# A decoder layer on one core: layer-norm scalings and hi/lo splits moved from VectorE to ScalarE, and a first body with an order of its own

## The chip, the core and the metric

The kernel runs on one core of one Trainium2 chip. The metric is the device time of one execution in microseconds. A core has TensorE (PE, with its weight loads as PEld), VectorE (DVE), ScalarE (ACT), GpSimd (POOL) and SyncE (SP, which here only issues DMAs). Each engine runs its own list of instructions in order and waits on semaphores.

## What is computed

x is 16 x 56 x 512 in float32, the context is 16 x 1500 x 512. Three residual blocks follow one another, each on a layer-normed x:

```python
x = x + attn(layernorm(x))           # 32 query heads, 8 key/value heads, causal, softmax
x = x + xattn(layernorm(x), ctx)     # latent cross-attention:
#   C_kv = ctx @ Wkv_d               (1500 x 32 per batch)
#   q    = (layernorm(x) @ Wq_d) @ W_qk      (16 heads x 32)
#   out  = softmax(q . C_kv / sqrt(32)) @ (C_kv @ Wv_u)
x = x + ffn(layernorm(x))            # x @ kernel + bias + two low-rank terms
# layernorm(x) = (x - mean) / sqrt(var + 1e-5)
```

## The kernel before

**Units of work.** Two batch elements form a pair (n = 0 to 7), since 2 x 56 rows fill the partitions. Pair n needs one self-attention, one set of cross-attention queries and one feed-forward. Each of the 16 batch elements b needs two passes of cross-attention. The first pass, `maxima(b, p)` on PE (line 754) with `reduce_piece` on DVE (line 1143), makes 21 pieces of scores and their row maxima. The maxima are negated (`NM`, lines 1148 to 1156, seven numbers per partition, split into a high and a low part), transposed (`MT`, line 637), copied by ACT into m_t and sent by two DMAs into rows 96 and 97 of the query operand q_st (`spread_m`, lines 341 and 343). The second pass, `scores(b, g, t)` (line 711), then gives scores with the maximum already subtracted: 24 units per batch element, in 6 groups g of 4. ACT takes the exponential of each unit into one of the 8 slots of p_ring (line 941), POOL adds the slots up into acc (line 1214), and `sums(b, g)` on PE multiplies a group with the context (line 726). The score banks are two (STB = 2), so a score matmul waits for the exponential two units earlier.

**Bodies and groups.** The program is one prologue and nine bodies i = 0 to 8. A body has 12 groups of instructions. In body i PE runs the scores of batch elements 2i-1 (groups 0 to 5) and 2i (groups 6 to 11), the pieces of 2i and 2i+1, and between them the small steps of the list `STEPS`, written out by hand: per group a list of names with a letter that says for which pair or batch element. All engines walk the same list and each does its part of a step. Within a group come first the four score units and the pieces of `PIECES_IN` (one per unit), with the sums of the group before after the second unit, then the steps. On ACT a group is first its four exponentials, then its parts of the steps.

**Steps of the change.** `Ah` and `A` (line 503) compute the transposed latent context C_kv of one batch element from ctx_sb into a PSUM bank. ACT copies the bank to ct_f (line 898, by the helper at line 840). `AS` on DVE makes ct_hl from ct_f: a rounded copy (line 1041) and the remainder (line 1043). SP spreads ct_hl into the operand c_st by 12 DMAs per batch element (`spread_ct`, line 393). `CT` (line 626) transposes ct_f for the sums. `L0`, `W1` and `YT` on DVE end in `statistics` (lines 1010 to 1014), which gives mean and variance; POOL's `power` makes rstd in two instructions (lines 1222 and 1225); `N0`, `N1` and `N2` on DVE normalise x into xn or x3n (line 1018); `T1`, `T2`, `T3` (line 490) transpose the result on PE, and ACT copies that into xnt. `K`, `Qh`, `Q1`, `WA`, `SA`, `WB`, `SB` are the self-attention's projections and scores, `SM0`/`SM1` (lines 1105, 1107), `SE0`/`SE1` (ACT, line 859) and `SN0`/`SN1` (lines 1115 to 1119) its softmax, `V`, `P0` to `P3`, `O1`, `Wh`, `W1` the rest of it; `CQ` and `H` make the cross queries, which SP spreads (line 402). `DN`, `DT`, `Y`, `YT` finish the cross-attention; `F1`, `Fh`, `F2` are the feed-forward.

**Loads.** SP reads the context of a batch element (3 MB, line 375) into one of two slots of ctx_sb. In the prologue it reads elements 0 and 1; element 2 is read at the start of body 0, element 3 after the spread of element 1. ACT issues half of the first queries' spreads (lines 335 to 336) and the two writes of the low-rank factors (line 985) before body 0.

**Line 1266 ff.** POOL's body is `power(0, i+1)`, then the additions of the bodies' units, with `power(1, i+1)` and `power(2, i-1)` between them.

## Time and profile before

| | us |
|---|---|
| median of 3 runs | 643.73 (642.36 to 645.56) |
| the profiled execution | 645.84 |
| its span | 644.0 |
| PE busy | 584.1 (91% of the span) |
| DVE busy | 432.5 (67%) |
| POOL busy | 412.7 (64%) |
| ACT busy | 302.1 (47%) |
| mean granted TensorE clock | 0.968 of full speed |

The profile is of one execution. The span goes from its first to its last instruction, and 1.84 us lie around it. A line of a timeline gives the start in us, the duration in us, the engine, the line of the program, the operation and its tiles, the number of instructions merged in it, and in brackets how long the engine had been idle and what released it. Busy PE time contains the overlap of following matmuls, so stalls are read from the brackets.

### The profile page before, as it was taken

How to read it: one execution, taken by the hardware profiler on the slowest of the kernel's cores; microseconds unless marked ns; L12 is line 12 of the kernel's file. 1: busy time of each engine (PE TensorE's matmuls, PEld its weight loads, DVE VectorE, ACT ScalarE, POOL GpSimd, SP SyncE). 2: the span in 40 equal slices, each digit the busy share in tenths (PEclk: the TensorE clock that was granted, in tenths of full speed). 3: DMA queues.
4: the chain of work that ended last, by engine and by line, in shares of the span. 5: the costliest groups of instructions: out<-in, count | busy, mean ns of one | idle time of the engine just before them, and what ended most of it. 6: DMA issues, size and time to landing. Idle time of an engine off the chain costs nothing.

```text
span 644.0 us, 11508 instructions
## 1 busy us (share of the span) xinstructions
PE 584.1 (91%) x4164; PEld 315.5 (49%) x4164; DVE 432.5 (67%) x715; ACT 302.1 (47%) x642; POOL 412.7 (64%) x385
## 2 busy tenths in 40 slices
PE   7889797998999899999999899998999899988887
PEld 7436353455446354545446355455446355434445
DVE  2737964678757967778747957678757967656632
ACT  1421434537444555437444555437444555464460
POOL 5002166598758887598758887588758887789000
PEclk9997788899999999999999999999999999999899
DMA  9959511651048110751039110761039110200000
GB/s 320 409 107 348 208 36 24 251 206 35 12 120 317 59 45 22 268 204 39 9 108 336 52 45 22 253 219 32 16 93 334 68 45 23 64 19 0 24 2 15
DMA packets 31578, 77.40 MB, mean 120 GB/s; under 512 B 11297, under 2 KB 24961, under 8 KB 29218
## 3 DMA queue, kind: packets, MB, share of 16 engines
q1 hardware_dynamic: 30854, 75.27, 34.9%
q10 hardware_dynamic: 668, 1.40, 0.6%
q8 instruction: 33, 0.54, 0.4%
q14 instruction: 23, 0.19, 0.1%
HBM read 58.92 MB, written 2.88 MB: 96 GB/s over the span
## 4 chain that ended last, share of the span: by engine, by line
PE 58%; DVE 19%; ACT 6%; POOL 4%; SPq 4%; issue 4%; DMA 4%; ACTq 0%; POOLq 0%; DVEq 0%
PE st_ps L711 11%; PE mx_ps L754 9%; PE pv_ps L726 8%; PE mi_ps L496 4%; PE mi_ps L490 4%; DVE mx_p L1143 4%; POOL acc L1214 3%; PE mi_ps L503 3%; DVE p L1066 2%; PE mi_ps L586 2%; SPq L402 2%; DMA ctx_sb<-in_ctx_t 2%; DVE xn L1018 2%; PE mi_ps L590 2%; DVE p L1107 2%
## 5 line engine op out<-in xcount | busy, mean ns | idle before, releaser
L1214 POOL TENSOR_TENSOR acc<-acc,p_ring 125x448 f32<-125x448 f32 x290 | 348.0, 1200 | 65.4 <-ACT p_ring L941 25.8
L1143 DVE TENSOR_REDUCE mx_p<-mx_ps 128x1 f32<-128x500 f32 x336 | 210.0, 669 | 98.9 <-PE mx_ps L754 97.9
L941 ACT ACTIVATE p_ring<-st_ps 125x448 f32<-125x448 f32 x372 | 183.4, 544 | 151.6 <-PE st_ps L711 139.7
L711 PE MATMUL st_ps<-q_st,c_st 98*125 98x448 f32 x372 | 146.3, 432 | 9.8 <-ACT p_ring L941 8.6
L754 PE MATMUL mx_ps<-c_st,q_st 96*128 96x500 f32 x336 | 142.1, 457 | 12.2 <-DVE mx_p L1143 5.1
L711 PEld LDWEIGHTS st_ps<-q_st,c_st 98*125 98x125 f32 x372 | 65.3, 190 | 99.3 <-ACT p_ring L941 79.9
L726 PE MATMUL pv_ps<-p_ring,c_nat 125*32 125x448 f32 x768 | 94.5, 564 | 1.9 <-ACT ox L840 1.0
L754 PEld LDWEIGHTS mx_ps<-c_st,q_st 96*128 96x128 f32 x336 | 63.6, 197 | 43.7 <-DVE mx_p L1143 17.6
L1222 POOL TENSOR_TENSOR rstd<-mv,eps_col 128x1 f32<-128x1 f32 x24 | 4.6, 190 | 117.1 <-DVE mv L1014 116.6
L503 PE MATMUL mi_ps<-ctx_sb,wkv_sb 128*32 128x375 f32 x480 | 46.8, 511 | 5.5 <-DVE p L1066 5.5
L1214 POOL TENSOR_TENSOR acc<-p_ring 125x448 f32<-125x448 f32 x29 | 35.6, 1226 | 19.2 <-ACT p_ring L941 19.2
L1098 DVE TENSOR_TENSOR x3n<-mi_ps,x 128x512 f32<-128x512 f32 x8 | 5.5, 692 | 46.0 <-PE mi_ps L695 46.0
L840 ACT ACTIVATE qt<-mi_ps 128x512 f32<-128x512 f32 x16 | 9.6, 598 | 48.8 <-PE mi_ps L496 44.0
L496 PEld LDWEIGHTS mi_ps<-xnt,wq_sb 128*128 128x128 f32 x256 | 31.1, 193 | 1.7 <-DMA wq_sb<-in_wq 0.8
L496 PE MATMUL mi_ps<-xnt,wq_sb 128*128 128x128 f32 x256 | 31.2, 276 | 0.6 <-DMA wq_sb<-in_wq 0.6
L726 PEld LDWEIGHTS pv_ps<-p_ring,c_nat 125*32 125x32 f32 x768 | 15.5, 109 | 30.4 <-issue 21.8
L859 ACT ACTIVATE p<-p 128x896 f32<-128x896 f32 x16 | 15.2, 951 | 26.4 <-DVE p L1107 26.4
L503 PEld LDWEIGHTS mi_ps<-ctx_sb,wkv_sb 128*32 128x32 f32 x480 | 13.1, 113 | 27.1 <-issue 18.2
L840 ACT ACTIVATE xnt<-mi_ps 128x512 f32<-128x512 f32 x24 | 14.3, 597 | 21.8 <-PE mi_ps L490 21.7
L1066 DVE TENSOR_TENSOR p<-mi_ps,cmask 128x448 f32<-128x448 f32 x32 | 18.4, 618 | 7.4 <-PE mi_ps L560 7.4
L490 PE MATMUL mi_ps<-ident,p 128*128 128x128 f32 x128 | 19.6, 289 | 3.5 <-ACT p1t L840 3.5
L1018 DVE TENSOR_SCALAR xn<-x_sb,mv,rstd 128x512 f32<-128x512 f32 x16 | 19.7, 1230 | 3.6 <-POOL rstd L1225 3.6
(137 smaller groups left out, 677.9 us busy)
## 6 DMA issues: line engine op xcount, KB each, us to landing
ctx_sb<-in_ctx_t SPq DMA_DIRECT2D x16, 3000.0 KB, 11.6
c_st<-ct_hl SPq DMA_DIRECT2D x192, 46.9 KB, 2.3
q_st<-q_hl SPq DMA_DIRECT2D x90, 56.0 KB, 2.0
x_sb<-in_x SPq DMA_DIRECT2D x8, 256.0 KB, 2.8
out_y<-x3n SPq DMA_DIRECT2D x16, 112.0 KB
wq_sb<-in_wq SPq DMA_DIRECT2D x2, 512.0 KB, 6.4
kern_sb<-in_lora_a SPq DMA_DIRECT2D x1, 1024.0 KB, 14.2
wo_sb<-in_wo SPq DMA_DIRECT2D x1, 1024.0 KB, 17.6
```

The costliest lines, as they stand in the source:

```text
L490: last = pe.transpose(bank_[:, c * 128:(c + 1) * 128], src[:, c * 128:(c + 1) * 128], ident[:, :])
L496: last = mm(o[:, r * 128:(r + 1) * 128], wq_sb[:, c, r * 128:(r + 1) * 128], xnt[:, c, :], start=(c == 0), stop=(c == CH - 1))
L503: last = mm(o[t * L:(t + 1) * L, 0:KT], wkv_sb[:, c, :], ctx_sb[:, slot, c, t * KT:(t + 1) * KT], start=(c == 0), stop=(c == CH - 1))
L711: mm(st_bank(unit)[0:KC, 0:HALF], c_st[:, b % 4, t * KT + k * KC:t * KT + (k + 1) * KC], q_st[:, b // 2 % 2, b % 2, half * HALF:(half + 1) ...
L726: last = mm(pv_ps[t * L:(t + 1) * L, 0:HALF], c_nat[:, b % 4, k, t * L:(t + 1) * L], p_ring[:, unit % PR, :], start=(k == 0), stop=(k == K ...
L754: mm(mx_ps[(b * PIECES + p) % MXB][:, 0:KP], q_st[0:96, b // 2 % 2, b % 2, j * 128:(j + 1) * 128], c_st[0:96, b % 4, k * KP:(k + 1) * KP], ...
L840: return act.activation(dst, src, ACT.Copy, scale=scale)
L941: act.activation(p_ring[:, unit % PR, :], st_bank(unit)[0:KC, 0:HALF], ACT.Exp, scale=float(L) ** -0.5).then_inc(exp_done, 1)
L1018: ve.tensor_scalar(dst, src, mv[:, which, 0:1], rstd[:, which, 1:2], ALU.subtract, ALU.mult)\
L1066: ve.tensor_tensor(rows[:, j:j + 2, half, :, 0:S], mi_ps[half][:, 0:G * S].rearrange("p (r g k) -> p r g k", r=2, g=G // 2), mask, ALU.add ...
L1143: ve.tensor_reduce(mx_p[:, p:p + 1], mx_ps[unit % MXB][:, 0:KP], AX.X, ALU.max).then_inc(red_done, 1)
L1214: po.tensor_tensor(dst, first, p_ring[:, unit % PR, :].rearrange("p (h s) -> p h s", s=S), ALU.add).then_inc(acc_done, 1)
```

## The change

- `statistics` gets a third result, the negated mean (one more DVE instruction of one element per partition), and `power` a third POOL instruction, -mean x rstd.
- `N0`, `N1`, `N2` run on ACT as one activation Identity with scale rstd and bias -mean x rstd; only `N0` and `N1` of pair 0, in the prologue, stay on DVE. `N0` keeps its place as the last step of group 0. `N1` stands in group 9 after the third exponential (in body 0 in group 7), `N2` in group 10 after the second.
- The rounded part of ct_hl is a second ACT copy from the bank of `A`; `AS` on DVE is only the remainder, and reads the bank. `AS` of the even batch elements moves from the end of group 5 to group 4, ahead of `SN0`. `CT` on PE waits for the remainder too.
- Body 0 gets its own list `FIRST_STEPS` and its own pieces. Batch element 0's scores start in group 4 (they started in group 6), groups 10 and 11 hold no steps, `Ah` and `A` of element 3 run on PE at the end of body 0 (they ran in group 0 of body 1). `MT` of element 0 uses a score bank, `Ah` and `A` of element 2 the bank of the sums.
- The context of element 2 is read from ACT's queue, behind ACT's spreads and the two writes.

```diff
-FIRST_PIECES_IN = [3, 2, 4, 0, 0, 0, 2, 4, 4, 0, 0, 0]
+FIRST_PIECES_IN = [3, 2, 4, 4, 0, 0, 4, 4, 4, 4, 0, 0]
...
-    [("SE0", "n"), ("Ah", "b"), ("MT", "m"), ("A", "b"), ("SE1", "n"), ("V", "n"), ("SN0", "n")],
-    [("CT", "b"), ("SN1", "n"), ("AS", "b")],
+    [("SE0", "n"), ("Ah", "b"), ("MT", "m"), ("A", "b"), ("AS", "b"), ("SE1", "n"), ("V", "n"),
+     ("SN0", "n")],
+    [("CT", "b"), ("SN1", "n")],
...
-    [("DN", "f"), ("Wh", "n"), ("M", 1), ("W1", "n"), ("M", 1), ("DT", "f"), ("N1", "n")],
-    [("YT", "f"), ("M", 1), ("T2", "n"), ("M", 1), ("CQ", "n"), ("M", 1), ("H", "n"), ("N2", "f")],
+    [("DN", "f"), ("Wh", "n"), ("M", 1), ("W1", "n"), ("M", 1), ("DT", "f")],
+    [("YT", "f"), ("M", 1), ("T2", "n"), ("M", 1), ("CQ", "n"), ("M", 1), ("H", "n")],
...
-FIRST_STEPS = {9: STEPS[9] + [("NM", "o")], 10: [("MT", "o")], 11: []}
+FIRST_STEPS = [
+    [("Ah", "a"), ("A", "a"), ("L0", "n"), ("M", 3), ("AS", "a"), ("N0", "n")],
+    [("CT", "a"), ("M", 1), ("T1", "n")],
+    [("K", "n"), ("M", 1), ("Qh", "n"), ("M", 3), ("Q1", "n")],
+    [("WA", "n"), ("NM", "m"), ("SA", "n"), ("Ah", "b"), ("MT", "m"), ("A", "b"), ("WB", "n"), ("SM0", "n"),
+     ("SB", "n"), ("SM1", "n")],
+    [("AS", "b"), ("SE0", "n"), ("V", "n"), ("CT", "b"), ("SE1", "n"), ("SN0", "n")],
+    [("SN1", "n"), ("P0", "n"), ("P1", "n"), ("P2", "n"), ("P3", "n")],
+    [("O1", "n"), ("M", 1), ("Wh", "n"), ("M", 1), ("W1", "n")],
+    [("M", 1), ("T2", "n"), ("M", 1), ("CQ", "n")],
+    [("H", "n"), ("M", 1)],
+    [("NM", "o"), ("MT", "o")],
+    [],
+    [],
+]
+FIRST_SCORES = 4
...
+def scores_at(i, g):
+    b, k = (2 * i - 1 + g // GROUPS, g % GROUPS) if i else (0, g - FIRST_SCORES)
+    return (b, k) if b < B and 0 <= k < GROUPS else None
+
+def sums_at(i, g):
+    if i == 0:
+        return scores_at(0, g - 1)
+    return None if (i, g) == (1, 0) else scores_at(*((i, g - 1) if g else (i - 1, 2 * GROUPS - 1)))
+
+N1_AT, FIRST_N1_AT = 9, 7
+
+def normal_at(i, g, t):
+    for (gn, tn), name, n in (((N1_AT if i else FIRST_N1_AT, 2), "N1", i + 1), ((10, 1), "N2", i - 1)):
+        if (g, t) == (gn, tn) and 0 <= n < PAIRS:
+            yield name, n
...
+            if n == 0 and name == "MT":
+                return st_ps[0]
+            if n == 2 and name in ("Ah", "A"):
+                return pv_ps
...
             def body(i):
-                if 2 * i + 2 < B:
-                    if i:
-                        load_x(i + 1)
+                if i and 2 * i + 2 < B:
+                    load_x(i + 1)
                     load_ctx(2 * i + 2)
...
                 elif name == "CT":
+                    if n == 2:
+                        pe.wait_ge(s1_sb, 8)
                     pe.wait_ge(a_f, n + 1)
+                    if n:
+                        pe.wait_ge(a_lo, n + 1)
...
                     for name, n in steps_of(i, g):
-                        if name in ("Ah", "A") and n == 1:
+                        if name in ("Ah", "A") and n in (1, 3):
                             continue
                         step(name, n, i, g)
                 if i == 0:
+                    for name in ("Ah", "A"):
+                        step(name, 3)
+                    pe.wait_ge(w_up, 16 * 4)
                     pe.wait_ge(w_ffn, 16 * 3)
                     pe.wait_ge(y_out, 16)
...
+            def normalise(which, n, src, dst):
+                act.wait_ge(ln_shift[which], n + 1)
+                act.activation(dst, src, ACT.Identity, bias=rstd[:, which, 2:3], scale=rstd[:, which, 1:2])\
+                    .then_inc(ln[which], 1)
...
                 elif name == "A":
+                    copy(ct_f[:, :], o[:, 0:KT]).then_inc(a_f, 1)
                     if n:
-                        act.wait_ge(a_lo, n)
-                    copy(ct_f[:, :], o[:, 0:KT]).then_inc(a_f, 1)
+                        act.wait_ge(cst_in[(n - 1) % 4], 16 * 12 * ((n - 1) // 4 + 1))
+                    copy(ct_hl[:, 0, :], o[:, 0:KT]).then_inc(a_hi, 1)
...
+            read_ctx(act.dma_start, 2)
             def body(i):
                 for g in range(2 * GROUPS):
-                    part, gg = g // GROUPS, g % GROUPS
-                    bs = 2 * i - 1 + part
-                    if 0 <= bs < B:
-                        exponentials(bs, gg)
...
+                    ready, summed = scores_at(i, g), sums_at(i, g)
+                    for t in range(4):
+                        if ready:
+                            exponential(*ready, t)
+                        for name, n in normal_at(i, g, t):
+                            step(name, n)
...
-                ve.bn_aggr(mv[:, which, :], stats[:, which, 0:6]).then_inc(s, 1)
+                ve.bn_aggr(mv[:, which, 0:2], stats[:, which, 0:6]).then_inc(s, 1)
+                ve.wait_ge(s, k + 2)
+                ve.tensor_scalar(mv[:, which, 2:3], mv[:, which, 0:1], -1.0, None, ALU.mult).then_inc(ln_neg[which], 1)
...
-                    if n:
-                        ve.wait_ge(cst_in[(n - 1) % 4], 16 * 12 * ((n - 1) // 4 + 1))
-                    ve.wait_ge(a_f, n + 1)
-                    ve.tensor_copy(ct_hl[:, 0, :], ct_f[:, :]).then_inc(a_hi, 1)
                     ve.wait_ge(a_hi, n + 1)
-                    ve.tensor_tensor(ct_hl[:, 1, :], ct_f[:, :], ct_hl[:, 0, :].bitcast(F32), ALU.subtract)\
+                    ve.tensor_tensor(ct_hl[:, 1, :], step_bank("A", n)[:, 0:KT], ct_hl[:, 0, :].bitcast(F32),
+                                     ALU.subtract)\
                         .then_inc(a_lo, 1)
...
                 po.tensor_tensor(rstd[:, which, 1:2], rstd[:, which, 0:1], minus_half[:, :], ALU.pow)\
                     .then_inc(ln_pow[which], 1)
+                po.wait_ge(ln_pow[which], n + 1)
+                po.wait_ge(ln_neg[which], n + 1)
+                po.tensor_tensor(rstd[:, which, 2:3], mv[:, which, 2:3], rstd[:, which, 1:2], ALU.mult)\
+                    .then_inc(ln_shift[which], 1)
```

## Rows read from the trace of the kernel before

**Rows 1.** The page, busy time of each engine over the span.

```profile
PE 584.1 (91%) x4164; PEld 315.5 (49%) x4164; DVE 432.5 (67%) x715; ACT 302.1 (47%) x642; POOL 412.7 (64%) x385
```

**Rows 2.** Windows, bodies 0, 1, 3, 4: length, busy PE PEld DVE ACT POOL, clock, DMA.

```profile
45.60:111.40 65.80, 53.80 (x312) 31.32 (x312) 47.35 (x78) 21.28 (x45) 25.54 (x23) 0.82 0.47 155
111.40:187.30 75.90, 71.81 (x499) 37.86 (x499) 52.24 (x85) 38.33 (x82) 59.57 (x54) 0.96 0.34 115
...
259.20:331.10 71.90, 67.81 (x498) 36.37 (x496) 52.76 (x86) 36.64 (x79) 55.38 (x51) 1.00 0.36 121
331.10:404.80 73.70, 69.52 (x498) 37.27 (x496) 53.03 (x86) 36.85 (x79) 55.36 (x51) 0.98 0.36 118
```

**Rows 3.** Timeline of PE in body 3, four rows before which it stood idle.

```profile
282.17 0.50 PE L754 MATMUL mx_ps<-c_st,q_st 96*128 96x500 f32 x1 [0.63 <-DVE p L1066]
...
286.23 1.47 PE L503 MATMUL mi_ps<-ctx_sb,wkv_sb 128*32 128x375 f32 x16 [0.57 <-DVE p L1066]
...
292.96 0.90 PE L711 MATMUL st_ps<-q_st,c_st 98*125 98x448 f32 x2 [0.92 <-ACT p_ring L941]
...
316.96 0.66 PE L490 MATMUL mi_ps<-ident,xn 128*128 128x128 f32 x4 [0.68 <-DVE xn L1018]
```

**Rows 4.** Groups of instructions over the whole span: count, busy us, mean ns, idle before.

```profile
L1018 DVE TENSOR_SCALAR xn<-x_sb,mv,rstd 128x512 f32<-128x512 f32 x16 | 19.7, 1230 | 3.6 <-POOL rstd L1225 3.6
...
L1043 DVE TENSOR_TENSOR ct_hl<-ct_f,ct_hl 128x375 fp32r<-128x375 f32 x16 | 15.1, 941 | 0.5
...
L840 ACT ACTIVATE x<-x_sb 128x512 f32<-128x512 f32 x8 | 5.0, 628 | 0.0
```

**Rows 5.** Timeline of body 3 around N0, end of group 0 and group 1.

```profile
265.72 0.48 ACT L840 ACTIVATE ct_f<-mi_ps 128x375 f32<-128x375 f32 x1 [2.72 <-PE mi_ps L503]
...
265.81 0.17 DVE L1014 BATCH_NORM_AGGREGATE mv<-stats 128x2 f32<-128x6 f32 x1
...
266.06 0.19 POOL L1222 TENSOR_TENSOR rstd<-mv,eps_col 128x1 f32<-128x1 f32 x1 [6.46 <-DVE mv L1014]
266.10 0.97 ACT L941 ACTIVATE p_ring<-st_ps 125x448 f32<-125x448 f32 x2
...
266.32 0.55 POOL L1225 TENSOR_TENSOR rstd<-rstd,minus_half 128x1 f32<-128x1 f32 x1
...
267.52 0.67 PE L711 MATMUL st_ps<-q_st,c_st 98*125 98x448 f32 x2
...
268.03 0.49 PE L626 MATMUL mi_ps<-ident,ct_f 128*125 128x128 f32 x3
```

**Rows 6.** Timeline of ACT in body 3, the four exponentials of group 5.

```profile
292.37 2.08 ACT L941 ACTIVATE p_ring<-st_ps 125x448 f32<-125x448 f32 x4
```

**Rows 7.** Timeline of body 3 around N1, group 9.

```profile
314.97 0.55 POOL L1225 TENSOR_TENSOR rstd<-rstd,minus_half 128x1 f32<-128x1 f32 x1
...
315.28 0.98 ACT L941 ACTIVATE p_ring<-st_ps 125x448 f32<-125x448 f32 x2 [0.51 <-PE st_ps L711]
```

**Rows 8.** Timeline of SP in body 0, the fourth context read and the first maxima sent.

```profile
59.06 0.58 SPq L375 DMA_DIRECT2D ctx_sb<-in_ctx_t  x1
71.73 1.63 SPq L341 DMA_DIRECT2D q_st<-m_t  x2
```

**Rows 9.** DMA issues from 59.0 to 60.5 us: KB each, us to landing.

```profile
ctx_sb<-in_ctx_t SPq DMA_DIRECT2D x1, 3000.0 KB, 16.0
```

**Rows 10.** Windows, two us at the start of body 1, columns as in rows 2.

```profile
112.00:114.00 2.00, 1.95 (x5) 1.24 (x5) 0.21 (x1) 1.54 (x3) 1.71 (x3) 0.50 0.36 84
```

**Rows 11.** Timeline of PE in body 0 and at the start of body 1, scores.

```profile
75.36 0.45 PE L711 MATMUL st_ps<-q_st,c_st 98*125 98x448 f32 x1
...
84.01 0.58 PE L711 MATMUL st_ps<-q_st,c_st 98*125 98x448 f32 x1
...
111.41 1.93 PE L711 MATMUL st_ps<-q_st,c_st 98*125 98x448 f32 x3 [2.05 <-ACT p_ring L941]
```

**Rows 12.** Waits over the whole span: us in total, times, longest us.

```profile
DVE x3n L1018 <- POOL rstd L1225: 3.8, 2, 2.9
```

More of the change, by code:

```diff
@@ L125, in steps_of @@
     done = sum(pieces_in(i)[g // GROUPS * GROUPS:g + 1])
-    done += sum(w for h in range(g // GROUPS * GROUPS, g) for name, w in STEPS[h] if name == "M")
+    done += sum(w for h in range(g // GROUPS * GROUPS, g) for name, w in steps_in(i, h) if name == "M")
     for name, w in steps_in(i, g):
@@ L160, in pieces_within @@
     done = sum(pieces_in(i)[g // GROUPS * GROUPS:g])
-    done += sum(w for h in range(g // GROUPS * GROUPS, g) for name, w in STEPS[h] if name == "M")
+    done += sum(w for h in range(g // GROUPS * GROUPS, g) for name, w in steps_in(i, h) if name == "M")
     return range(done, done + pieces_in(i)[g])
@@ L280, in decoder_layer @@
         ln_pow = [sem(f"ln_pow{n}") for n in range(3)]
+        ln_neg = [sem(f"ln_neg{n}") for n in range(3)]
+        ln_shift = [sem(f"ln_shift{n}") for n in range(3)]
         st_done = sem("st_done")
@@ L614, in step @@
                 elif name == "Ah":
-                    if n % 2 == 0 and n:
+                    if n % 2 == 0 and n > 2:
                         pe.wait_ge(s1_sb, 2 * n + 4)
@@ L720, in sums @@
                     pe.wait_ge(ct_sb, b + 1)
+                if b == 0 and g == 0:
+                    pe.wait_ge(a_f, 3)
                 if k == 0 and b * 2 + half:
@@ L922, in step, with exponential @@
                     copy(ax_t[0:2 * RANK, :], o[0:2 * RANK, 0:128]).then_inc(f1_sb, 1)
-            def exponentials(b, g):
-                half = g // KG
-                if b == 0 and g == 0:
+            def exponential(b, g, t):
+                unit = b * 24 + g * 4 + t
+                if unit == 0:
                     act.wait_ge(eff_out, 32)
-                for t in range(4):
-                    unit = b * 24 + g * 4 + t
-                    act.wait_ge(st_done, unit + 1)
-                    old = unit - PR
-                    if old >= 0:
-                        act.wait_ge(pv_done, old // 4 + 1)
-                        added = (old // 24, old // 12 % 2)
-                        if added in DVE_HALVES:
-                            act.wait_ge(acc_dve, dve_adds(*added) + max(old % 12, 1))
-                        elif added != PE_HALF:
-                            act.wait_ge(acc_done, pool_adds(*added) + max(old % 12, 1))
-                    act.activation(p_ring[:, unit % PR, :], st_bank(unit)[0:KC, 0:HALF], ACT.Exp,
-                                   scale=float(L) ** -0.5).then_inc(exp_done, 1)
+                act.wait_ge(st_done, unit + 1)
+                old = unit - PR
+                if old >= 0:
+                    act.wait_ge(pv_done, old // 4 + 1)
+                    added = (old // 24, old // 12 % 2)
+                    if added in DVE_HALVES:
+                        act.wait_ge(acc_dve, dve_adds(*added) + max(old % 12, 1))
+                    elif added != PE_HALF:
+                        act.wait_ge(acc_done, pool_adds(*added) + max(old % 12, 1))
+                act.activation(p_ring[:, unit % PR, :], st_bank(unit)[0:KC, 0:HALF], ACT.Exp,
+                               scale=float(L) ** -0.5).then_inc(exp_done, 1)
             def out_of_sums(b, half):
```

64 lines of the change are left out of this document (39 added, 25 removed).

## The prediction

> **What bounds the kernel now.** I read the page first, then the windows body by body, then PE's timeline of one body, then the stretches of the other engines that release it. By the page TensorE is busy 91% of the span and DVE 67% [rows 1], so work taken from DVE is worth only what PE waits for it. The windows show two regimes [rows 2]. Body 3 stands for bodies 2 to 6: 71.9 us, PE busy 67.8, clock 1.00, so some 4 us of stalls each. Bodies 0 and 1 are worse: 65.8 us at a mean clock of 0.82 with 12 us of PE idle, and 75.9 us at 0.96, which is 4.0 longer than body 3. The first body and the entry to the second are where time lies; a steady body has stalls of half a microsecond.
>
> In body 3 the stalls that matter here are before four rows [rows 3]: 0.63 and 0.57 us for the masks' additions of the softmax, 0.92 for the exponentials of group 5, 0.68 for N1's xn. Only the last is a wait for an operation that the change moves. The others keep their releasers.
>
> **What the moved work costs.** On DVE a normalisation takes 1230 ns in the mean, the remainder 941; an ACT pass over 128x512 in SBUF takes 628 [rows 4]. Per steady body DVE sheds N0, N1 and N2, 3.7 us of 52.8, and two CASTs. I price that at nothing by itself: DVE is idle 19 us of a steady body and PE waits for it only at the rows named. It costs something if DVE's work after the moved ones was late for PE; no bracket in body 3 shows that in groups 0 to 2. The added negation on DVE is hidden by POOL's power chain.
>
> **N1, each steady body.** POOL's second instruction ends at 315.52 [rows 7]. The new third one is of the form of the first, 0.19 long and 0.26 after its predecessor with its semaphore [rows 5], so the shift is there at 315.78. ACT starts the third exponential at 315.28 and is free some 0.44 later, so N1 runs from about 315.85 to 316.48 and T2 starts at 316.54 instead of 316.96 [rows 3]. The fourth exponential slips by 0.6, behind YT and T2 on PE, and nothing waits. Gain 0.42 us per body.
>
> **N0, each steady body: a new wait.** N0 is now ahead of group 1's four exponentials in ACT's order. Before, ACT went from the ct_f copy at 265.72 straight to the first exponential at 266.10 [rows 5]. Now the second copy for ct_hl takes that place, and ACT is free at 266.5. N0 waits for POOL: the aggregate ends at 265.98, POOL's second instruction at 266.87, the third at 267.13 [rows 5]. N0 starts at 267.2, and the next ACT instruction 0.52 later (the 628 of rows 4 less some 0.1 of overlap): the first exponential at 267.72 instead of 266.10. A queued exponential is followed by its score matmul 0.59 us after its start: 292.37 [rows 6] and 292.96 [rows 3]. So the third score starts at 268.31 instead of 267.52 [rows 5]. The fourth waits for the second exponential, 0.44 later, 268.75, and CT, 0.27 after it, starts at 269.02 instead of 268.03. PE loses 1.0 us. Bounds: 0 if POOL were so early that the first exponential still started by 266.93; 1.2, what the same pattern cost in group 5 (0.92 and a spacing 0.2 longer). I take 1.0, since every term is a row. Behind ACT nothing else suffers: the CT copy and T1's copy shift by the same 1.0, and POOL's additions start 0.26 later.
>
> **The splits.** In group 4 the second copy falls where ACT waited for SM1, so SE1 and V keep their times. AS in group 4 puts 0.9 us at most [rows 4] ahead of SN0, and PE has group 5's scores and sums before P0 and P2 need SN0 and SN1. SP's 12 DMAs start 5 us earlier; their consumer is a body away. CT's wait for the remainder ends before CT in both halves. All these: 0, at worst 0.3 per body.
>
> **The first body.** Its start is unchanged: DVE reduces the pieces one by one. In the new order T1, K, Q1 come within half a microsecond of where they were, and with all 21 pieces of element 0 ahead of SA, m_t can be issued at about 65.5 by my count instead of 71.73 [rows 8]. But its two DMAs stand on SP's queue behind the fourth context, which was issued at 59.06 and took 16.0 us to land, 75.06 [rows 8, 9], while the first score started at 75.36 [rows 11]. With the third context on ACT's queue SP issues the fourth some 1.6 us earlier (the start of element 1's spread no longer waits for DVE's CAST; my estimate), with the same bytes to move. I put the first scores at 73.5. From there: it was 8.65 us to the next score group at 84.01 [rows 11]; in the new order one more group of four exponentials, 2.08 [rows 6], stands in it, while part of the softmax is done before, 9.5 by my count. From there to body 1 it was 27.4. One group with its sums less is -3.0; five pieces more are +1.2 (an estimate, a piece behind a score costs about half of its 0.50 [rows 3]); Ah and A of element 3 are two times 1.47 [rows 3], +2.9; N1 on ACT is -0.7; the stall of 2.05 before body 1, ACT busy with issuing m_t's DMAs [rows 11], is covered by those Ah and A: 25.8, with a wait for m_in of 0.2. Body 1 would start at 109.0; PE has been idle for five us before 73.5, after which I expect the clock at its lower level for some of group 4, +1.0. So 110.0, 1.4 earlier.
>
> **Body 1** loses Ah and A: 2.9 us at the full clock, up to twice that at the 0.50 that PE had just after the entry [rows 10]; I take 3.3. Body 1 is 4.0 us longer than body 3 [rows 2], which I put down to that clock. With a shorter stall at the entry I take back about half of the remaining 3.6, less a little for doubt: -1.5.
>
> **The end.** The two last N2 wait for POOL [rows 12]; each becomes 0.26 + 0.08 later, +0.6 together.
>
> **Sum**: -1.4 (body 0), -3.3 and -1.5 (body 1), +6.0 (N0, bodies 1 to 6), -2.5 (N1, the same six), +0.6 (end): -2.1 us. The profiled execution took 645.84, 2.1 above the median of 643.73. Against it the sum gives 643.7, against the median 641.6, which is what I forecast. Half a percent, 3.2 us, is about what a measurement of this kernel can tell from no change; the forecast lies inside it.
>
> **Two rules weighed.** The two context reads now lie on two queues. In the trace the third, ahead in one queue, had landed before its use. The Trainium skill, "DMA: Bandwidth & Descriptors", section on queues, rings and completion order, says that each DMA engine goes round-robin between the queues that have work. By it the third context lands later, since the fourth takes half the rate from 57.4 on. That would hold Ah of element 2 by up to 2 us. It falls into the wait for m_t, so the sum stays. The same section says that a DMA's semaphore lands only after every earlier write of that DMA engine, across its queues. By it m_t's rows can't be ahead of the fourth context, and the next rival is excluded; no row of before shows it.
>
> **Rivals.**
> *m_t's rows don't wait* for the fourth context. For: they are 7 KB. Against: 3 MB stand ahead of them in their queue. Then SP's issue from 65.5 to 67.1 and 2 us of landing put the first scores at 69.1: 4.4 earlier, -6.5, 637.2. With the clock full in body 1 it is 1.8 less, 635.4.
> *N0's wait is hidden*, if POOL or the x load is earlier than in body 3: the sum loses 6.0 and is -8.1, 635.6. Against: L0's place in DVE's list is unchanged.
> *The clock falls in the steady bodies* (slower). Body 4 took 73.7 us at a mean clock of 0.98, 1.8 more than body 3 [rows 2]. A fall of that size after the new 1.0 us idle in group 1, in each of the five other bodies 1 to 6, is +9.0, and the sum +6.9, 650.6. It decides from three bodies on (+3.3). For: PE's idle share rises by 1.4% and the falls in bodies 0 and 1 come after stalls. Against: 0.92 and 0.57 close together didn't bring it in body 3.
> *DVE's relief does nothing and body 0 keeps its length*: without -1.4 and -1.5 the sum is +0.8, 644.5.
>
> **How the numbers follow.** Forecast 0.45, own range 638.5 to 645 by the bounds of N0 (0.6 to 1.2 us a body), of body 0 (2 us either way) and of the clock. m_t early 0.18, N0 hidden 0.07, clock 0.17, no gain 0.13. Faster by over 0.5% are the two fast rivals and a third of the forecast: 0.40. Slower by over 0.5% are the clock rival and a little of the others: 0.20. The rest 0.40. The range takes in the fast rivals at 635 and the clock rival in four bodies, 649.
>
> **What would show it.** Per body, right: PE idle before the third score of group 1, released by the exponential behind xn; T2's idle near 0.25; body length 72.5. First score near 73.5, behind the fourth context; body 1 starting near 110 and near 71 long. Wrong: steady bodies under 71.9 (N0 mispriced), a first score before 71, or windows with a clock under 1.00 in bodies 2 to 6.

## The result, and the profile of the changed kernel

The changed kernel takes 649.17 us (median of 5 runs, 648.3 to 650.07), the kernel before 644.93 (median of 5, 642.36 to 646.46): 1.0072 times as long, 95% interval 1.0046 to 1.0098. It is slower by 4.2 us, where 2.1 faster was forecast. The profiled executions stand 2.5 us apart (648.3 and 645.84): the one of before lies 0.9 above its median, the other 0.9 below. The balance by stages below is of these two profiles; 1.7 of the 4.2 us between the medians it can't show.

The page's busy times, which answer to [rows 1]:

```profile
PE 577.3 (89%) x4164; PEld 313.9 (49%) x4164; DVE 404.4 (63%) x701; ACT 323.8 (50%) x680; POOL 416.3 (64%) x409
```

DVE has shed 28 us, ACT took 22 more, and PE stands idle for 9 us more than before (span less busy time). The windows of bodies 0, 1, 3 and 7, in the columns of [rows 2]:

```profile
46.00:114.00 68.00, 52.79 (x354) 30.75 (x355) 43.24 (x76) 25.10 (x52) 31.05 (x29) 0.90 0.46 154
114.00:185.30 71.30, 65.62 (x455) 36.49 (x456) 48.30 (x83) 39.44 (x83) 54.75 (x53) 0.98 0.35 117
258.60:331.20 72.60, 68.14 (x498) 36.49 (x496) 49.03 (x84) 39.66 (x84) 55.40 (x54) 1.00 0.37 120
549.80:609.00 59.20, 52.11 (x295) 24.10 (x293) 36.96 (x64) 30.12 (x63) 39.83 (x37) 0.91 0.08 21
```

Taking the start of body 1's first scores and the start of the last matmul of each pair's F2 as marks, the time stands like this (us; bodies 2 to 6 are five lengths from mark to mark):

| stretch | before | after | difference | forecast |
|---|---|---|---|---|
| to body 1's first scores | 112.63 | 114.00 | +1.4 | -1.4 |
| body 1 | 73.8 | 71.3 | -2.6 | -4.2 |
| bodies 2 to 6 | 362.1 | 363.8 | +1.7 | +2.9 |
| body 7 | 57.6 | 59.1 | +1.4 | together |
| behind it | 33.3 | 33.8 | +0.5 | +0.6 |

(Body 1's forecast is -3.3 and -1.5, with one body's share of N0 and N1, +0.6.) In the kernel before, body 1 starts at 112.63 and not at 111.41, which the prediction takes from [rows 11] for it. The windows of that kernel, with its score matmuls (L711) alone, tell it; the numbers after x are their counts on PE and PEld:

```profile
75.30:111.40 36.10, 8.46 (x22) 4.08 (x22) 0.91 0.10 24
75.30:112.62 37.32, 9.63 (x24) 4.57 (x25) 0.90 0.11 26
```

Element 0 has 24 scores, and only 22 lie before 111.41. That row is the third score of the last group of body 0, and the stall of 2.05 us before it stands inside body 0. The prediction's start of body 1, 110.0, is therefore 111.2 by the true mark; its differences stay. The largest miss is the first body, 2.8 us. The timeline of PE there in the changed kernel, for [rows 11]:

```profile
75.91 1.11 PE L766 MATMUL st_ps<-q_st,c_st 98*125 98x448 f32 x2 [6.91 <-DMA q_st<-m_t]
...
109.56 0.27 PE L692 MATMUL mi_ps<-ident,nm_hl 128*14 128x128 f32 x1 [1.83 <-DVE nm_hl L1232]
...
114.00 0.45 PE L766 MATMUL st_ps<-q_st,c_st 98*125 98x448 f32 x1 [0.76 <-DMA q_st<-m_t]
```

PE stands still for 6.91 us before the first scores, and waits for the two rows of m_t. The timeline of SP and, below, one row of the chain, for [rows 8]:

```profile
59.26 0.58 SPq L387 DMA_DIRECT2D ctx_sb<-in_ctx_t  x1
67.01 1.61 SPq L393 DMA_DIRECT2D q_st<-m_t  x2
...
67.90 7.97 DMA q_st<-m_t
```

m_t is issued at 67.01, 4.7 us earlier than before, but 7 KB take 7.97 us to land: the fourth context, issued at 59.26, takes 16.3 us and lands at 75.5. Of a steady body, the groups 0 and 1 of body 3, for [rows 5]:

```profile
265.28 0.48 ACT L901 ACTIVATE ct_f<-mi_ps 128x375 f32<-128x375 f32 x1 [2.72 <-PE mi_ps L553]
...
265.89 0.55 POOL L1301 TENSOR_TENSOR rstd<-rstd,minus_half 128x1 f32<-128x1 f32 x1
...
266.51 0.19 POOL L1305 TENSOR_TENSOR rstd<-mv,rstd 128x1 f32<-128x1 f32 x1
...
266.74 0.81 ACT L905 ACTIVATE xn<-x_sb,rstd 128x512 f32<-128x512 f32 x1 [0.61 <-POOL rstd L1305]
267.46 0.96 ACT L1012 ACTIVATE p_ring<-st_ps 125x448 f32<-125x448 f32 x2
...
268.04 0.90 PE L766 MATMUL st_ps<-q_st,c_st 98*125 98x448 f32 x2 [0.89 <-ACT p_ring L1012]
```

This is the forecast's picture: ACT waits for POOL's third instruction, N0 stands ahead of the exponentials, and PE loses 0.89 us before the third score.

### The profile page after: what moved, and what is told of

It is laid out like the page before. It is cut to its first block, busy times and chain, and to the rows that moved or that the text cites. A ratio compares the mean times of both kernels' runs of the same rounds, so it can differ in the third digit from the quotient of the medians.

```text
span 646.5 us, 11585 instructions
## 1 busy us (share of the span) xinstructions
PE 577.3 (89%) x4164; PEld 313.9 (49%) x4164; DVE 404.4 (63%) x701; ACT 323.8 (50%) x680; POOL 416.3 (64%) x409
## 3 DMA queue, kind: packets, MB, share of 16 engines
q1 hardware_dynamic: 30710, 72.19, 33.8%
## 4 chain that ended last, share of the span: by engine, by line
PE 56%; DVE 17%; ACT 7%; issue 6%; DMA 6%; POOL 5%; SPq 2%; ACTq 1%; POOLq 0%; DVEq 0%
PE st_ps L766 11%; PE pv_ps L783 8%; PE mx_ps L811 8%; POOL acc L1290 4%; DVE mx_p L1219 4%; PE mi_ps L546 3%; PE mi_ps L540 3%; ACT p_ring L1012 3%; DMA ctx_sb<-in_ctx_t 3%; PE mi_ps L637 2%; DVE p L1183 2%; PE mi_ps L641 2%; PE mi_ps L744 2%; DVE p L1138 2%; DVE sm L1181 2%
## 5 line engine op out<-in xcount | busy, mean ns | idle before, releaser
L766 PE MATMUL st_ps<-q_st,c_st 98*125 98x448 f32 x372 | 148.3, 435 | 23.1 <-ACT p_ring L1012 14.3
L811 PE MATMUL mx_ps<-c_st,q_st 96*128 96x500 f32 x336 | 140.2, 448 | 11.2 <-DVE mx_p L1219 4.8
L766 PEld LDWEIGHTS st_ps<-q_st,c_st 98*125 98x125 f32 x372 | 65.9, 190 | 113.2 <-ACT p_ring L1012 87.7
L1290 POOL TENSOR_TENSOR acc<-p_ring 125x448 f32<-125x448 f32 x29 | 33.1, 1142 | 20.6 <-ACT p_ring L1012 20.6
L553 PE MATMUL mi_ps<-ctx_sb,wkv_sb 128*32 128x375 f32 x448 | 40.6, 483 | 0.0
L783 PEld LDWEIGHTS pv_ps<-p_ring,c_nat 125*32 125x32 f32 x768 | 15.4, 108 | 30.3 <-issue 23.8
L1195 DVE TENSOR_TENSOR p<-p,sm 128x896 f32<-128x896 f32 x16 | 22.5, 1408 | 0.6
L1191 DVE TENSOR_REDUCE sm<-p 128x16 f32<-128x896 f32 x16 | 17.2, 1077 | 7.1 <-ACT p L931 7.0
L540 PE MATMUL mi_ps<-ident,p 128*128 128x128 f32 x128 | 17.9, 275 | 4.0 <-ACT p1t L901 3.6
## 6 DMA issues: line engine op xcount, KB each, us to landing
ctx_sb<-in_ctx_t ACTq DMA_DIRECT2D x1, 3000.0 KB, 16.9
```

What stands on the lines that cost most here:

```text
L540: last = pe.transpose(bank_[:, c * 128:(c + 1) * 128], src[:, c * 128:(c + 1) * 128], ident[:, :])
L553: last = mm(o[t * L:(t + 1) * L, 0:KT], wkv_sb[:, c, :], ctx_sb[:, slot, c, t * KT:(t + 1) * KT], start=(c == 0), stop=(c == CH - 1))
L766: mm(st_bank(unit)[0:KC, 0:HALF], c_st[:, b % 4, t * KT + k * KC:t * KT + (k + 1) * KC], q_st[:, b // 2 % 2, b % 2, half * HALF:(half + 1) ...
L783: last = mm(pv_ps[t * L:(t + 1) * L, 0:HALF], c_nat[:, b % 4, k, t * L:(t + 1) * L], p_ring[:, unit % PR, :], start=(k == 0), stop=(k == K ...
L811: mm(mx_ps[(b * PIECES + p) % MXB][:, 0:KP], q_st[0:96, b // 2 % 2, b % 2, j * 128:(j + 1) * 128], c_st[0:96, b % 4, k * KP:(k + 1) * KP], ...
L1191: ve.tensor_reduce(total, rows, AX.X, ALU.add).then_inc(soft_n, 1)
```

## The experiments

Eleven kernels were run, each timed against the kernel before. Ratios are to that kernel, with 95% intervals; they are not the quotients of the medians and differ from them by up to 0.003 (b3: 633.79 over 644.50 would be 0.983). "Mean of bodies 2 to 6" is that of the five lengths between F2 marks in the profile: 72.77 for the changed kernel and 72.43 for before (its median is 72.12, since one of the five was lengthened by a clock fall). The labels are those of the headings.

**a1, the fourth context behind m_t.**

```diff
-                            if n % 2 and n + 2 < B:
+                            if n % 2 and n + 2 < B and n != 1:
                                 load_ctx(n + 2)
...
                                 spread_m(dma, n)
+                            if n == 0:
+                                load_ctx(3)
```

> The changed kernel with one read moved on SyncE's queue: the fourth context (ctx element 3) is issued behind the two DMAs that spread m_t of element 0, and no longer ahead of them. Changed kernel: 649.2 us, 1.0072 times the kernel before; its first scores start at 75.9. Theory 1 (the first scores wait in the queue for the 3 MB context ahead of m_t): first scores near 69.5, PE's idle time before them under 1.5 us in place of 6.9, body 1 starts 5 to 6 us earlier than 114.0, about 643.5 us in all (ratio 0.998). The fourth context then lands later (near 84), which its use in front of body 1 still covers. Theory 2 (the rows of m_t are late for another reason, or the time is given back at the next wait of the first body): first scores early but body 1 at 113 to 114, 648.5 to 649.5 us (ratio 1.006 to 1.007). Theory 3 (the semaphore of m_t also waits for the other queue's context): first scores near 74, 647 us.

Measured: 642.54 us (12 runs), ratio 0.9982 (0.9952 to 1.0012). PE and SP in the first body, and the window of body 1:

```profile
69.86 0.67 PE L768 MATMUL st_ps<-q_st,c_st 98*125 98x448 f32 x2 [0.73 <-DMA q_st<-m_t]
...
67.14 1.60 SPq L393 DMA_DIRECT2D q_st<-m_t  x2
68.78 0.43 SPq L387 DMA_DIRECT2D ctx_sb<-in_ctx_t  x1
...
108.80:178.50 69.70, 64.13 (x459) 35.17 (x456) 48.26 (x83) 39.10 (x83) 54.70 (x53) 1.00 0.35 118
```

m_t is issued at the same time, and the first scores start at 69.86 in place of 75.91. Body 1 starts at 108.81, 5.2 earlier, so 0.9 of the 6.1 us is given back before it. It is also 1.6 shorter, at a clock of 1.00 in place of 0.98, but that isn't the edit's: b1 and b2, with the read ahead of m_t, show 69.7 us for it too. The numbers are those of theory 1: the read ahead of m_t is what held the first scores.

**a2, N0 behind the second exponential of group 1.**

```diff
-    [("Ah", "a"), ("M", 2), ("L0", "n"), ("M", 1), ("A", "a"), ("AS", "a"), ("N0", "n")],
+    [("Ah", "a"), ("M", 2), ("L0", "n"), ("M", 1), ("A", "a"), ("AS", "a")],
...
-    for (gn, tn), name, n in (((N1_AT if i else FIRST_N1_AT, 2), "N1", i + 1), ((10, 1), "N2", i - 1)):
+    for (gn, tn), name, n in (((N1_AT if i else FIRST_N1_AT, 2), "N1", i + 1), ((10, 1), "N2", i - 1),
+                              ((1, 1) if i else (0, 9), "N0", i + 1)):
```

> The changed kernel with the first normalisation (N0) of bodies 1 to 6 moved on ScalarE from the end of group 0, ahead of group 1's four exponentials, to behind the second exponential of group 1. Changed kernel: 649.2 us, ratio 1.0072. Theory 1 (ScalarE's wait for GpSimd's chain in front of those exponentials costs 0.9 to 1.0 us in each of six bodies): steady bodies of 71.8 to 72.0 us in place of 72.6 to 73.0, 643.7 us in all (ratio 0.999). Theory 2 (the steady bodies are longer for another reason: the additional ScalarE copy ahead of CT, or DVE's and GpSimd's contention): steady bodies stay at 72.6 or above, 648.5 to 649.5 us (ratio 1.006 to 1.007). A mixed case, where T1 becomes the next wait because xn comes 1 us later: 646 us.

Measured: 643.12 us (12 runs), ratio 0.9981 (0.9961 to 1.0002); mean of bodies 2 to 6 71.70, 1.07 less. ACT and PE around N0 in body 3:

```profile
261.15 0.99 ACT L1013 ACTIVATE p_ring<-st_ps 125x448 f32<-125x448 f32 x2
...
262.21 0.68 PE L767 MATMUL st_ps<-q_st,c_st 98*125 98x448 f32 x2
...
262.46 0.81 ACT L906 ACTIVATE xn<-x_sb,rstd 128x512 f32<-128x512 f32 x1 [0.33 <-POOL rstd L1306]
...
263.33 0.66 PE L541 MATMUL mi_ps<-ident,xn 128*128 128x128 f32 x4
```

No stall stands before the score, and T1 (L541) finds xn ready although ACT still waits 0.33 for POOL. Theory 1 holds.

**a3, N2 of the last two pairs back on DVE.** Behind YT and without its negation and third POOL instruction:

```diff
+                elif name == "D2" and n in N2_ON_DVE:
+                    normalise(2, n, x3[:, :], x3n[:, :])
```

> The changed kernel with the third normalisation (N2) of the last two pairs alone back on DVE at its old place, without their negation and GpSimd's third instruction. Changed kernel: 649.2 us, ratio 1.0072; its body 7 took 59.2 us and what follows it 37.5, 1.4 and 0.5 more than before. Theory 1 (moving N2 off DVE lets DVE's additions run beside GpSimd's power chain, which gets slower by it, and a third instruction and a ScalarE pass of 0.81 us are longer than DVE's own): body 7 near 57.8 and the rest near 37.0, 647.2 us in all (ratio 1.004). Theory 2 (the end is longer because of the clock that PE has there, not because of N2): within 0.3 us of 649.2 (ratio 1.007).

Measured: 649.12 us (6 runs), ratio 1.0087 (1.0059 to 1.0116). The total shows no gain. What follows body 7 took 33.3 us from mark to mark, as before, in place of 33.8, but body 7 took 59.6: in it the four matmuls of Fh (L746) took 3.61 us in place of 1.98, at the lower clock. In the profiles of all kernels here body 7 took 57.6 to 59.6 us with that N2 on DVE (8 profiles, mean 58.3), and 59.1 to 60.4 with it on ACT (5 profiles, mean 59.8). The run neither shows the 2 us nor excludes a smaller part of them.

**a4, the three edits together.**

> The three edits of the runs before together: the fourth context behind m_t's spread, N0 behind the second exponential of group 1, N2 of the last two pairs back on DVE. If the three terms add up (5.5, 5.5 and 2 us by the theories 1 of the single edits): 636 us, 0.987 times the kernel before, faster than both. If one of them is given back at another wait: 641 to 643 us (0.994 to 0.998). If the terms share a cause, such as the clock, the sum of the single gains is missed by over 2 us.

Measured: 635.56 us (6 runs), ratio 0.9880 (0.9852 to 0.9907): faster than both kernels. The ratios of a1 and a2 give 0.9982 x 0.9981 / 1.0072 = 0.9892 by themselves, so the two terms add up, and 0.8 us is left for N2, which is less than the interval's half, 1.8 us. Of the end, first the changed kernel, then a4; DVE's additions of the accumulator are L1213 and L1222:

```profile
594.46 1.15 DVE L1213 TENSOR_TENSOR acc<-p_ring 125x448 f32<-125x448 f32 x1
...
595.72 2.10 DVE L1213 TENSOR_TENSOR acc<-acc,p_ring 125x448 f32<-125x448 f32 x2
596.56 0.57 POOL L1298 TENSOR_TENSOR rstd<-mv,eps_col 128x1 f32<-128x1 f32 x1
...
597.21 1.01 POOL L1301 TENSOR_TENSOR rstd<-rstd,minus_half 128x1 f32<-128x1 f32 x1
...
598.30 0.19 POOL L1305 TENSOR_TENSOR rstd<-mv,rstd 128x1 f32<-128x1 f32 x1
598.52 0.81 ACT L905 ACTIVATE x3n<-x,rstd 128x512 f32<-128x512 f32 x1 [3.36 <-POOL rstd L1305]
```

```profile
583.47 0.19 POOL L1307 TENSOR_TENSOR rstd<-mv,eps_col 128x1 f32<-128x1 f32 x1
583.73 0.55 POOL L1310 TENSOR_TENSOR rstd<-rstd,minus_half 128x1 f32<-128x1 f32 x1
...
584.32 0.55 DVE L1100 TENSOR_SCALAR x3n<-x,mv,rstd 128x512 f32<-128x512 f32 x1 [2.90 <-POOL rstd L1310]
584.78 0.62 DVE L1222 TENSOR_TENSOR acc<-p_ring 125x448 f32<-125x448 f32 x1
```

While N2 was DVE's, DVE waited for POOL there and its additions came behind. Off DVE, the additions run beside POOL's two small instructions, and both suffer: 0.57 and 1.01 in place of 0.19 and 0.55, 1.05 to 1.15 for an addition in place of 0.62 to 0.67. From the aggregate's end to the start of N2 it is 5.9 us, and 4.6 in a4.

**b1, m_t of element 0 from ACT's queue.** The changed kernel, the fourth context left ahead on SP's:

```diff
-                            if n != 1:
+                            if n > 1:
...
-                    if n == 1:
+                    if n <= 1:
```

> The changed kernel with the two DMAs that spread m_t of element 0 issued from ScalarE's queue, where the third context (landed at 64.97) is all that stands ahead of them; the fourth context stays where the change has it, ahead on SyncE's queue, and moves its bytes at the same time. Changed kernel: m_t issued at 67.0, first scores at 75.91, ratio 1.0072. Theory 1 (a DMA waits for what stands ahead in its own queue only): first scores at 69.5 to 71, ratio about 0.998, as in the run that moved the context. Theory 2 (the completion of a DMA waits for earlier writes of the same DMA engines, whichever queue they are of): first scores stay near 75.5 to 76, ratio 1.007. In between, if the engines only share their rate by turns: 71 to 73, ratio about 1.001.

Measured: 650.95 us (10 runs), ratio 1.0088 (1.0051 to 1.0125). The chain and PE:

```profile
65.70 1.33 ACTq L393
67.06 7.23 DMA q_st<-m_t
...
74.34 1.11 PE L766 MATMUL st_ps<-q_st,c_st 98*125 98x448 f32 x2 [6.66 <-DMA q_st<-m_t]
```

m_t is issued 1.3 us earlier here than in the profile of the changed kernel, and needs 7.23 us in place of 7.97, in a queue in which nothing unfinished stood ahead. Theory 1 falls: the order within the queue isn't the cause. The first scores lie between theory 2 (75.5 to 76) and the case in between (71 to 73). The fourth context itself landed only at 58.53 + 18.1 = 76.6, so m_t doesn't wait for all of it either. The Trainium skill, "DMA: Bandwidth & Descriptors", section on queues, rings and completion order, says that a semaphore lands only after every earlier write of its DMA engine, across its queues. The run agrees with it in part. The trace records each packet of a transfer: m_t's 14 rows of 512 bytes start at 69.73 to 72.44 here, the last one 5.4 us after the second DMA's issue began, where in a1 (68.60 to 69.44) it is 1.4; and m_t lands 1.9 us after its last row starts, in a1 0.4. So of the 5.4 us by which this landing takes longer than a1's 1.8, some 3.9 are rows that themselves come late beside the context's packets of 24000 bytes, and only 1.5 can be a wait for earlier writes. Why the rows come late no run separates.

**b2, the third context back on SP's queue.**

```diff
-                if i and 2 * i + 2 < B:
-                    load_x(i + 1)
+                if 2 * i + 2 < B:
+                    if i:
+                        load_x(i + 1)
                     load_ctx(2 * i + 2)
...
-            read_ctx(act.dma_start, 2)
```

> The changed kernel with the third context's read issued by SyncE behind the weights of the last stage, as in the kernel before, in place of ScalarE's queue. Changed kernel: it is issued at 48.04 and lands at 64.97, PE waits 0.76 for it, ratio 1.0072. Theory 1 (the reads share one rate, and the queue it lies in decides little): lands between 61 and 66, first scores within 0.5 us of 75.9, because the fourth context still ends last; ratio 1.006 to 1.008. Theory 2 (on two queues the third context gets half the rate while the fourth runs): back in one queue it lands near 60, A of element 2 and m_t are not held, but the first scores stay at the fourth context's end, 75 to 76. Rival: the additional DMA on SyncE delays the 12 transfers of the effective latents, and the first scores are over 1 us later, ratio 1.009.

Measured: 649.42 us (10 runs), ratio 1.0064 (1.0035 to 1.0092). The context lands at 49.78 + 16.09 = 65.9, first scores at 76.82. In the one queue it takes 16.1 us, in ACT's 16.9 (48.04 to 64.97 in the changed kernel), and 16.1 in b1, on ACT's too: the queue of this read decides nothing that shows, and theory 2 (near 60) falls. The first scores are 0.9 later than in the changed kernel, where theory 1 allowed 0.5; the fourth context is issued 0.8 later here, at 60.03.

**b3, a4 with N1 of pairs 2 to 7 back on DVE.**

```diff
+                elif name == "D1":
+                    normalise(1, n, x2_sb[:, slot, :], xn[:, :])
```

> The version with the three edits together, with the second normalisation (N1) of pairs 2 to 7 back on DVE at its place in the kernel before, without their negation and GpSimd's third instruction. The three edits together: ratio 0.988, steady bodies of 71.5 to 72.2 (mean 71.9). By the prediction's term N1 on ScalarE saves 0.42 us in each of six bodies: steady bodies of 72.2 to 72.4, 638.1 us (ratio 0.992). Rival (T2's wait was no longer the bound, or the fourth exponential's delay gives it back): steady bodies as they are, ratio 0.988.

Measured: 633.79 us (4 runs), ratio 0.9803 (0.9753 to 0.9852); mean of bodies 2 to 6 71.75, against 71.94 in a4. The prediction's term for N1 falls. Groups 9 and 10 of body 3, first a4 (N1 on ACT), then b3; the last two rows of a4 are weight loads of PE:

```profile
306.70 0.66 PE L545 MATMUL mi_ps<-ident,xn 128*128 128x128 f32 x4 [0.20 <-ACT xn L910]
...
307.03 2.69 POOL L1299 TENSOR_TENSOR acc<-acc,p_ring 125x448 f32<-125x448 f32 x2
307.04 1.68 DVE L1179 TENSOR_TENSOR x<-x3n,x 128x512 f32<-128x512 f32 x1
...
310.56 0.19 PEld L816 LDWEIGHTS mx_ps<-c_st,q_st 96*128 96x128 f32 x1 [0.39 <-DVE mx_p L1228]
...
311.14 0.19 PEld L816 LDWEIGHTS mx_ps<-c_st,q_st 96*128 96x128 f32 x1 [0.29 <-DVE mx_p L1228]
```

```profile
305.54 1.14 POOL L1301 TENSOR_TENSOR acc<-p_ring 125x448 f32<-125x448 f32 x1
305.61 1.36 DVE L1100 TENSOR_SCALAR xn<-x_sb,mv,rstd 128x512 f32<-128x512 f32 x1 [0.20 <-POOL rstd L1312]
...
307.02 0.66 PE L545 MATMUL mi_ps<-ident,xn 128*128 128x128 f32 x4 [0.68 <-DVE xn L1100]
...
306.82 2.69 POOL L1301 TENSOR_TENSOR acc<-acc,p_ring 125x448 f32<-125x448 f32 x2
...
307.60 0.91 DVE L1181 TENSOR_TENSOR x<-x3n,x 128x512 f32<-128x512 f32 x1
```

On ACT, T2 does start earlier, by 0.25 us counted from the body's start. But DVE's next pass with its inputs in SBUF now starts together with one of POOL's additions and takes 1.68 us in place of 0.91; the statistics, the negation and three maxima stand behind it, and the pieces of group 10 wait 0.39 and 0.29 for their bank, where b3's show no such wait. From the matmuls on wqd_sb, which follow T2, to the end of the body it is 12.5 us in a4 and 12.0 in b3.

**b4, a4 with the latents of element 3 back in body 1.**

```diff
-                        if name in ("Ah", "A") and n in (1, 3):
+                        if name in ("Ah", "A") and n == 1:
...
-                    for name in ("Ah", "A"):
-                        step(name, 3)
```

> The version with the three edits together, with the latents of element 3 (Ah and A, 32 matmuls) back in body 1 instead of the end of the first body. The three edits together: ratio 0.988, body 1 (from its first scores, 108.75, to the last matmul of its F2, 176.52) takes 67.8 us at a clock of 1.00. Theory 1 (they fill a stall at the entry, ScalarE busy with m_t's DMAs and the query's transfers late): body 1's first scores come only 0.8 to 1.5 us earlier, body 1 is 2.9 to 3.3 longer, +2 us in all (ratio 0.991). Theory 2 (moved work costs the same in either place): body 1's first scores 2.9 earlier, body 1 2.9 longer, ratio 0.988. Theory 3 (without them the clock falls in body 1, as in the kernel before): body 1 over 72 us and a clock under 0.98, ratio 0.994.

Measured: 639.34 us (9 runs), ratio 0.9905 (0.9868 to 0.9942). At the entry to body 1 PE shows this, with the windows of 108 to 112 of b4 and, last, of a4:

```profile
108.48 0.71 PE L771 MATMUL st_ps<-q_st,c_st 98*125 98x448 f32 x1 [2.69 <-DMA q_st<-m_t]
...
108.00:112.00 4.00, 3.52 (x11) 2.26 (x15) 2.04 (x3) 2.03 (x4) 0.00 (x0) 0.50 0.74 208
```

```profile
108.00:112.00 4.00, 3.91 (x24) 1.90 (x16) 2.51 (x5) 2.61 (x6) 0.00 (x0) 1.00 0.68 205
```

The scores start 0.3 earlier than in a4, since PE waits 2.69 us for m_t, and body 1 takes 73.0 us in place of 67.8: 2.9 for the latents at the full clock and 2.3 more, with the clock at 0.50 after the wait (to 114.8; the latents' two halves take 2.73 and 1.47 us). In all it is 3.8 us between the medians, 1.6 by the ratios. Theories 1 and 3 both hold in part.

**c1, everything back on DVE**: a4 with N0, N1 and N2 of all later bodies on DVE. **c2**: the same with N0 on ACT as in a2.

> The new first body, the splits that read PSUM, and the fourth context behind m_t's spread, but all three normalisations of pairs 2 to 7 (N2 of all pairs) back on DVE at their places in the kernel before: of the change's move of normalisations to ScalarE only N0 and N1 of pair 1 are left. Theory 1 (taking the normalisations off DVE is worth nothing in a steady body, because DVE's passes wait for GpSimd's additions wherever they stand, and the relief turns up as the next wait): steady bodies of 71.5 to 72.0, as with N0 late and N1 on DVE (mean 71.75), ratio 0.978 to 0.984. Theory 2 (DVE's relief by N0 and N2 is what makes those bodies short): steady bodies at 72.3 or more, ratio 0.986 or more.

> The fastest version so far (three edits together and N1 on DVE, ratio 0.980, steady bodies 71.75 in the mean), with N2 of the first six pairs on DVE too; ScalarE keeps N0 behind the second exponential of group 1. Theory 1 (no one waits for N2 in a steady body, and without its negation DVE's pieces in group 10 come 0.2 earlier): steady bodies of 71.5 to 71.8, ratio 0.978 to 0.982. Theory 2 (DVE's 1.2 us for N2 in group 10 makes the pieces of the next groups wait): steady bodies of 72.2 or more, ratio 0.985.

Measured: c1 635.1 us (6 runs), 0.9857 (0.9832 to 0.9881); four of its five bodies take 71.45 to 71.82, the fifth 72.98, at a clock of 1.00, and no run explains it. c2 633.08 us (6 runs), 0.9837 (0.9809 to 0.9865), mean of bodies 2 to 6 71.84. The expected ratios of c1 and c2 were missed a little upwards, but the body lengths are those of theory 1 in both: these runs tell no difference between normalisations on DVE and on ACT.

**c3, the kernel before with the fourth context behind m_t.** The edit is that of a1.

> The kernel before with one read moved on SyncE's queue: the fourth context behind the two DMAs of m_t of element 0 and ahead of the effective latents of element 1. Before: m_t issued at 71.73, first scores at 75.36, body 1 from 111.41. If m_t's rows wait for the context there too: first scores at 73.9 to 74.3, 1.2 us earlier, ratio 0.998 if it is kept. Rival: the spread of element 1's effective latents, issued at 79.2, now shares with the context until 85 and the pieces of element 1 come late, so that body 1 starts at 111.4 or later: ratio 0.999 to 1.003. Against the changed kernel with the same edit (0.998) this tells what the new order of the first body brings by itself: its first scores came at 69.86.

Measured: 644.42 us (12 runs), ratio 1.000 (0.998 to 1.002). m_t is issued at 72.93 there, the first scores start at 75.67, body 1 at 112.8 (112.6 before). The scores follow m_t's issue by 2.7 us in place of 3.6, but m_t is issued 1.2 later, in a body that stands 0.8 later as a whole (the third context is issued at 49.60 in place of 48.77). No gain shows in the time. In the old order m_t is issued at 71.73, 3.3 us before the context lands, so little of the read is left to wait for: the negated maxima are ready at 67.2, and their transpose stands behind the latents on PE until 71.0.

## Why the prediction was wrong

The direction failed on one step, the first body: its miss of 2.8 us alone turns the forecast of -2.1 into +0.7. Body 1 missed by 1.7 more, and the other two misses nearly cancel (-1.2 and +1.4).

**The first scores: the step that failed.** The prediction had m_t issued at 65.5 (67.01 measured) and saw that its rows stand behind the fourth context. It took the context to be issued 1.6 us earlier than [rows 8] and put the first scores at 73.5. It was issued 0.2 later, at 59.26: SP's 12 transfers ahead of it did start 1.2 earlier, but took 9.5 us in place of 8.1. The scores came at 75.91: +2.4 us. (In a2, a3 and b2, with the same order, the context is issued at 57.7 to 60.9 and the scores come at 75.2 to 79.1, so this isn't the profile's accident.) The whole gain of the new order, 5.5 us from 75.36 to the 69.86 of a1, stayed locked up behind that read. The rival in which m_t doesn't wait named the right size (69.1) for the case without the read. That m_t can't land ahead of the read was named too; b1 bears it out in effect, but shows that more goes on than an order of completion. The third context, by the first of the two rules weighed up to 2 us late, held PE for 0.76, and that did fall into the wait for m_t.

**From there to body 1**: 38.1 us in place of 36.5. Of the 1.6, 1.2 is the wrong mark: the prediction counted up to the 23rd score and left the last two out. The stall of 2.05 that it covered with the latents of element 3 stood inside the last group. At the true entry b4 shows that the latents do stand where PE would wait 2.7 us for m_t, but in the changed kernel PE waits 1.83 for the negated maxima and then 0.76 for m_t, where 0.2 was left for it. No run splits the rest of this term.

**Body 1**: -2.6 against -4.2. By the true mark body 1 was 2.8 us longer than body 3 and not 4.0, so there was less clock to win back. The latents are priced right, at 3.3: they took 1.97 and 1.47 us there in the kernel before. With +0.6 for N0 and N1 that leaves nothing for the clock, where -1.5 was forecast, since in this profile the clock fell inside the body:

```profile
121.80:125.00 3.20, 3.20 (x12) 2.86 (x13) 0.68 (x1) 2.24 (x5) 2.77 (x4) 0.50 1.04 338
```

In a1, b1 and b2 it fell before the body's first scores and stayed at 1.00 in it; there body 1 takes 69.7 us, -4.2. The size of the term is right in those, and where the fall comes isn't the same in each kernel.

**N0: right.** Forecast +1.0 a body; in body 3 PE's idle time is 0.89 and 0.9 is still there at the masks' stall of group 3 (24.7 us into the body in place of 23.8); 1.07 by a2. The size of the ACT pass was off: 0.81 us, not the 0.63 of [rows 4], with its next instruction 0.72 later instead of 0.52. The Trainium skill, "ScalarE: Activation LUTs", section on what ACT_TABLE_LOAD costs, adds some 0.09 us for each per-partition operand; scale and bias here are two, and the 0.19 between 814 and 628 ns agrees.

**N1: wrong, but small.** T2's idle time became 0.20 as forecast (0.25), and the prediction said that nothing waits behind it. Something did, on DVE: its next pass in SBUF met an addition of POOL, and from group 10 on 0.5 was lost. Net +0.2 a body in place of -0.42, by b3.

**The splits**: forecast 0. The stall of 0.57 before the latents [rows 3] went away in the changed kernel, some 0.3 a body. With N0 and N1 this makes the +0.7 that body 3 shows (72.6 against 71.9), close to the +0.6 forecast: the sum was right by two misses.

**The end**: +0.6 forecast, +2.0 in the profiles. The prediction priced the additional POOL instruction (0.34 a time) but not that DVE, no longer waiting, would run its additions beside POOL's chain. How much of the 2.0 that is stays open, by a3.

**DVE's relief was priced at nothing**, which c1 bears out. The reason given, that no one waits for DVE, was only half of it: a part was never relief. The two groups in which most of it comes back, first in the kernel before, then in the changed one:

```profile
L1119 DVE TENSOR_TENSOR p<-p,sm 128x896 f32<-128x896 f32 x16 | 17.5, 1092 | 0.6
...
L1094 DVE TENSOR_TENSOR x<-x3n,x 128x512 f32<-128x512 f32 x8 | 6.8, 854 | 0.3
```

```profile
L1195 DVE TENSOR_TENSOR p<-p,sm 128x896 f32<-128x896 f32 x16 | 22.5, 1408 | 0.6
...
L1170 DVE TENSOR_TENSOR x<-x3n,x 128x512 f32<-128x512 f32 x8 | 10.5, 1310 | 0.3
```

5.1 and 3.6 us were given back, and 1.5 by the softmax's other pass over 128x896 (1132 to 1224 ns).

**The slower rival**, a clock fall in the steady bodies, didn't happen: bodies 2 to 6 show 72.6 to 73.0 us, and the clock is 1.00 from 125.2 to 592.7. The chance of 0.20 for slower lay on the wrong mechanism. What decided was a step that the prediction had, the wait for a read in front of m_t, taken 2.4 us too lightly.

So the change is three things: a new order up to the end of body 1 that is worth 7.5 to 11 us with the read behind m_t (that end lies at 178.9 in c1, 176.5 in a4 and 175.4 in c2, at 186.5 before), a read placed so that it takes some 6 of them back, and a move to ScalarE that costs 6 to 8 us where N0 and N2 stand and brings nothing that these runs can tell where they stand well.

## What to carry to other kernels

Before a small transfer that PE waits for, look for a large read in either queue: moving the 3 MB read behind the 7 KB was worth 5.8 us here, moving the 7 KB to the other queue nothing. Where a stage ends is worth a count: a stall taken for the entry to body 1 stood two scores before it. When a pass goes to another engine, look at what stands behind it in the new engine's order (here four exponentials, 1 us a body), and at what the relieved engine now runs at the same time as its neighbour. A new order and a move between engines belong in separate kernels: the order, once the read stood behind m_t, made this kernel 1.4% faster (c1), and in the change the read's place and N0's hid it.
